# A graph layer's edge loop in which TensorE signals its results by a drain instead of by an increment at the product

## The reference

```
h = relu(layernorm(x))                                  # 12500 nodes x 128
rbf  = cut(d) * sin(k*pi*d/6) / (k*pi*d/6),  k = 1..8   # 200000 edges
w    = silu(silu(rbf @ fc_w1) @ fc_w2) @ fc_w3          # 4 x 32 weights for each edge
gs, gv = lin1(h)[src]                                   # gather: a row of 128 for each edge
msg  = [w00*gs*sh0, w11*(gv.sh1)/sqrt(3), w01*gs*sh1, w10*gv*sh0]    # 256 columns
agg  = segment_sum(msg, dst) / count                    # dst is sorted
out  = x + sc(h) + tanh(agg_s @ alpha_w) * lin2(agg)
```

## Time and profile before

| | |
|---|---|
| median of 3 timed runs | 2211.73 us (2203.23 to 2214.47) |
| profiled execution, first to last instruction | 2483.8 us |
| PE busy / weight loads busy | 1811.4 us (73%) / 1174.2 us (47%) |
| DVE busy | 1783.0 us (72%) |
| ACT busy | 1199.1 us (48%) |
| POOL busy | 1578.4 us (64%) |
| mean granted TensorE clock | 0.826 of 2.4 GHz |

### The profile page before, as it was taken

One profiled execution on the slowest core, in us unless ns is written; L12 is line 12 of the kernel. 1 busy time (PEld: TensorE's weight loads), 2 busy tenths in 40 slices (PEclk: granted clock), 3 DMA queues, 4 the chain that ended last, 5 costly groups with the idle time before them and its releaser, 6 DMA issues. The chain is left out here.

```text
span 2483.8 us, 34021 instructions
## 1 busy us (share of the span) xinstructions
PE 1811.4 (73%) x7969; PEld 1174.2 (47%) x7969; DVE 1783.0 (72%) x4669; ACT 1199.1 (48%) x3310; POOL 1578.4 (64%) x1624
## 2 busy tenths in 40 slices
PE   6577777787777777767677767667787776877777
PEld 6344444454444444444444434444554444544544
DVE  8577767767776777767676667767677776777777
ACT  6354545455454555444444344445444444445443
POOL 7566666666666666666666666666666666666563
PEclk9588878878888887788787878888888888888889
DMA  7322222222222222222122222222222222222222
GB/s 214 70 64 67 56 64 66 66 56 66 66 59 62 67 65 56 55 48 50 46 50 48 48 48 49 54 50 64 57 67 62 59 65 66 53 64 61 59 66 55
DMA packets 347699, 155.73 MB, mean 63 GB/s; under 512 B 237983, under 2 KB 322048, under 8 KB 347584
## 3 DMA queue, kind: packets, MB, share of 16 engines
q0 software_dynamic: 50016, 102.51, 15.7%
q1 hardware_dynamic: 296938, 51.75, 11.4%
q10 hardware_dynamic: 630, 0.29, 0.0%
HBM read 134.27 MB, written 20.15 MB: 62 GB/s over the span
## 5 line engine op out<-in xcount | busy, mean ns | idle before, releaser
L970 POOL DMA_INDIRECT lin_g<-lin_table,src_ix x1563 | 1530.0, 979 | 865.1 <-issue 441.5
L1157 ACT ACTIVATE lin_sh<-lin_g,harm 128x128 f32<-128x128 f32 x1563 | 483.8, 396 | 94.6 <-DMA lin_g<-lin_table,src_ix 87.6
L1040 PE MATMUL ps_sums<-near_sums,far_hot 128*128 128x257 f32 x520 | 208.0, 488 | 440.8 <-DVE agg L1474 206.0
L1030 PE MATMUL ps_near<-msg,onehot 128*64 128x257 f32 x3126 | 507.5, 471 | 1.2 <-DVE msg L1423 1.2
L1018 PE MATMUL ps_w<-w,h 128*128 128x256 f32 x1566 | 462.6, 440 | 28.2 <-ACT key_all L1167 18.5
L1018 PEld LDWEIGHTS ps_w<-w,h 128*128 128x128 f32 x1566 | 395.3, 272 | 135.4 <-issue 44.9
L999 PE MATMUL ps_h<-rbf,w 32*128 32x192 f32 x1044 | 277.0, 390 | 138.0 <-issue 67.1
L1415 DVE TENSOR_TENSOR msg<-lin_sh,key_all 128x576 f32<-128x576 f32 (+1 forms) x261 | 197.3, 756 | 249.9 <-ACT key_all L1167 209.5
L1167 ACT ACTIVATE key_all<-ps_w 128x768 f32<-128x768 f32 x261 | 213.5, 818 | 305.2 <-remote 188.6
L1030 PEld LDWEIGHTS ps_near<-msg,onehot 128*64 128x64 f32 x3126 | 241.3, 164 | 230.6 <-issue 175.7
L1383 DVE TENSOR_TENSOR lin_sh<-lin_g,ps_meta 128x576 f32<-128x576 f32 (+1 forms) x261 | 196.6, 753 | 212.2 <-DMA lin_g<-lin_table,src_ix 207.0
(11 more groups left out here) (175 smaller groups left out, 1655.2 us busy)
## 6 DMA issues: line engine op xcount, KB each, us to landing
lin_g<-lin_table,src_ix POOLq DMA_INDIRECT x1563
dist_in<-in_edge_weight SPq DMA_DIRECT2D x67, 96.0 KB
lin_table<-lin_out SPq DMA_DIRECT2D x24, 256.0 KB, 2.6
x_in<-in_x SPq DMA_DIRECT2D x24, 256.0 KB
skip_table<-x_in SPq DMA_DIRECT2D x24, 256.0 KB
xq<-in_x SPq DMA_DIRECT2D x23, 256.0 KB, 3.9
harm<-in_edge_attr SPq DMA_DIRECT2D x66, 48.0 KB
x_in<-skip_table SPq DMA_DIRECT2D x8, 256.0 KB
```

The costliest lines, as they stand in the source:

```text
L970: pool.indirect_dma_start(slot_tiles(s, u)[rows, t, :], None, lin_table, bass.IndirectOffsetOnAxis(ap=src_ix[rows, s.phase, u, col:col + 1 ...
L1030: mm = pe.matmul(ps_near[half * NEAR:(half + 1) * NEAR, 0:MSG + 1], onehot[:, u, t, :], msg[:, u % 2, t, :], start=(j == 0), stop=(j == PA ...
L1040: pe.matmul(ps_nodes(i), far_hot[:, u, :], near_sums[:, u % 2, :], start=True, stop=True).then_inc(sums_ready, 1)
L1157: last = act.activation(lin_sh0[:, u % 2, j, :], slot_tiles(s, u)[:, j, :], ACT.Copy, scale=harm[:, s.phase, u, harm_col(j):harm_col(j) + 1])
```

## The change

The five increments move from the last matmul of their part to a drain that follows it. Everything else stays: the products, their order, the waits, the semaphores and who waits for them. There are five drains for each group, 1305 in the edge loop. The order of the matmuls on TensorE, and of all instructions on the other engines, is the same as before.

```diff
@@ layer1
                             for part in range(2):
-                                mm = pe.matmul(ps_h1[:, part * SEG:(part + 1) * SEG], w1[rows, 2 * k + part, :], rbf[rows, :],
+                                pe.matmul(ps_h1[:, part * SEG:(part + 1) * SEG], w1[rows, 2 * k + part, :], rbf[rows, :],
                                                start=True, stop=True)
-                            mm.then_inc(h1_done, 1)
+                            pe.drain(fusable=False).then_inc(h1_done, 1)
@@ layer2
-                            pe.matmul(ps_h2[:, 0:UNIT], w2[:], h1[:, k % 2, :], start=True, stop=True).then_inc(h2_done, 1)
+                            pe.matmul(ps_h2[:, 0:UNIT], w2[:], h1[:, k % 2, :], start=True, stop=True)
+                            pe.drain(fusable=False).then_inc(h2_done, 1)
@@ layer3
                             for j in range(PAIRS):
-                                mm = pe.matmul(ps_w[:, 2 * j * P:(2 * j + 2) * P], cols[:, j, :], w3[:], start=True, stop=True)
-                            mm.then_inc(w_ready, 1)
+                                pe.matmul(ps_w[:, 2 * j * P:(2 * j + 2) * P], cols[:, j, :], w3[:], start=True, stop=True)
+                            pe.drain(fusable=False).then_inc(w_ready, 1)
@@ near_layer
-                                    mm = pe.matmul(ps_near[half * NEAR:(half + 1) * NEAR, 0:MSG + 1], onehot[:, u, t, :], msg[:, u % 2, t, :],
+                                    pe.matmul(ps_near[half * NEAR:(half + 1) * NEAR, 0:MSG + 1], onehot[:, u, t, :], msg[:, u % 2, t, :],
                                                    start=(j == 0), stop=(j == PAIRS - 1))
-                            mm.then_inc(near_ready, 1)
+                            pe.drain(fusable=False).then_inc(near_ready, 1)
@@ segment_sum
-                            pe.matmul(ps_nodes(i), far_hot[:, u, :], near_sums[:, u % 2, :], start=True, stop=True).then_inc(sums_ready, 1)
+                            pe.matmul(ps_nodes(i), far_hot[:, u, :], near_sums[:, u % 2, :], start=True, stop=True)
+                            pe.drain(fusable=False).then_inc(sums_ready, 1)
```

## The result

The changed kernel takes 2276.8 us (median of 4 runs, 2267.28 to 2281.96) against 2211.62 us of the kernel before (the median once a fourth run is counted): a ratio of 1.029, with a 95% interval of 1.026 to 1.0325, or 65 us more. The forecast was 2312 us, with 2120 to 2450 as its range.

The account below looks back on a forecast made before the run. POOL was taken to set the pace at full clock, PE at half clock. Uncovered half-clock drains (129 us) plus 10 us for late results, scaled by 0.89 and rounded down to 100, gave 2211.73 + 100 = 2312 us, range 2120 to 2450.

Parts of the forecast that it names:

- (a): PE's stream at full clock: drained parts no longer overlap, 5.40 us a group in place of 4.86, +0.54 us.
- (b): PE, ahead of layer3 and segment_sum: weight loads no longer run ahead of their products, +0.22 us a group.
- (c): PE, each drain: the drain itself and the sequencer's restart take 0.10 us, +0.5 us a group (0.2 to 1.5).
- 92 groups at half clock x 1.4 us: Edge loop: 92 of 261 groups run at half clock, where nothing covers the drains' 1.4 us each; 129 us.
- the loss sits at half clock: Edge loop: drains are hidden at full clock (4.9 to 6.1 us a group, under POOL's 7.5) and cost time at half clock.
- POOL as the cover: Edge loop at full clock: POOL's six gathers take 7.5 us a group and hide PE's longer group; cover 1.4 us.
- floor of 2051 us: POOL: 1563 gathers at 1.25 us make 1954 us, plus 68.1 us ahead of the first and 29.4 from the last's start.
- Rival 1: PE's signals arriving after their modelled end also slow timed runs, and drains end these late signals; 2130 us, chance 0.22.
- ACT's "remote" waits: Sign: ACT's idle waits ended by "remote" events, 342.1 and 188.6 us, should shrink if the signal comes from the sequencer.
- Rival 2: No change: PE runs nearly always at full clock and the 1.26 us hide behind POOL; 2205 to 2222 us, chance 0.11.
- Rival 3: Much slower: the drains' gaps cost PE its clock, half clock for 60% of the groups; 2555 us, chance 0.12.
- Rival 4: Drains' signals come as late as the increments did, with PE stopped meanwhile; timed runs as forecast, chance 0.55 shared with it.

Follow-up runs that it names:

- one_drain: Kernel before plus one silent drain an iteration, behind the last part of its fourth group, all increments left at the products; ratio 1.005 to the kernel before.
- layers_only: Kernel before with signalling drains behind layer1, layer2 and layer3 only; near_layer and segment_sum keep their increments at the products; ratio 1.033 to the kernel before.
- unpaced_before: Kernel before without POOL's waits for h2_done and sums_ready ahead of a group's third and fifth gather; 2181.5 us, ratio 0.986 to the kernel before.
- half_gather_before: Kernel before with all loop gathers but the first four groups' and the last fetching 64 of 128 rows; 2196.2 us, ratio 0.992 to the kernel before.
- layer2_twice: Kernel before with layer2's product issued twice into the same place, no drain; 2277.2 us, ratio 1.029 to the kernel before.

## Why the prediction was right, and where it was not

- **Direction and range: right.** Slower was given 0.66, and the time lies in the range, 35 us under the forecast.
- **(a) Parts end to end, +0.54 us: held.** In the changed kernel no product behind a drain starts less than 0.079 us after the modelled end of the one ahead.
- **(b) Weight loads in the open: held.** They start with their product. The first products of layer3 stretch its 1.46 us to 1.62 and those of segment_sum its 0.60 to 0.67: 0.23 us where 0.22 stood.
- **(c) 0.10 us for a drain and the restart: too small in two places.** The drain is 0.08 us. But ahead of segment_sum and of layer1 the gap is 0.22 us. There a second wait or register work stands in PE's list; in one_drain the next part starts 0.07 to 0.16 us before the modelled end all the same, so the sequencer did this while earlier products ran. The sum is 1.46 us at full clock instead of 1.26.
- **92 groups at half clock x 1.4 us: right in kind, with a wrong count.** The 1.4 us held: the distances between the parts at half clock make 10.93 us where they made 9.46 (the 9.40 us of the earlier trace rows is the length of the window), +1.47. The number of groups came from a disturbed execution. Undisturbed, 2 x (1 - 0.858) x 2226.0 = 632 us pass at half clock before, 67 groups, and 2 x (1 - 0.909) x 2280.2 = 415 us after, 38 groups. 38 x 1.47 = 56 us is near the 65 measured, but that is in part luck: the same product gives 49 us for layers_only, which costs 72.
- **Why 1.46 us x 261 = 381 us in PE's stream are only 65 us at the end.** PE's idle time from 100 us of the span on is nearly the same in both (466 and 448 us), but its gaps of more than 2 us sum up to 347 us in one_drain and to 166 in the changed kernel, and the stretches at half clock fell from 99 to 72. The 217 us less at half clock are worth at most half of that, some 109 us, and PE's wait for DVE's sum is 173.6 us shorter. Both are estimates of what is given back; they leave some 100 us where the spans differ by 54, so the account isn't closed. That it is the spread of the idle time that holds the clock is argued, not shown.
- **That the loss sits at half clock: only in part.** Sorting DVE's waits at L1416 (one_drain) and L1417 (changed) of over 0.1 us by the mean clock of the 7 us before them, those under 0.75 sum up to 54 us in one_drain and 73 after, those between to 38 and 62, those above 0.97 to 2 and 17. So 15 of the 58 us more fall where the prediction had the drains hidden.
- **POOL as the cover: wrong engine.** This step failed, though the time came out in the range. With POOL's two waits gone and with shorter gathers the drains cost 1.030 and 1.034, where a cover by POOL would have made them dearer (1.05 or more was expected). The loss shows on DVE, busy for 78 to 80% of the span, and PE gives up 173.6 us of its own wait for DVE. That these two are the cover is argued from the waits. The fastest kernel here still stands 130 us above the floor of 2051 us.
- **Rival 1 (faster) rested on the late signals, and these were no part of the kernel.** My reason for giving it little weight, that the profiled execution was 272 us longer than the median, was the right sign. None of the kernels run later shows a "remote" wait, three of them without any drain (unpaced_before, half_gather_before, layer2_twice). So that ACT's "remote" waits are gone in the changed kernel tells nothing of the drain, as I had thought it would.
- **Rival 2** fell with the result. **Rival 3** (the clock collapses) had the sign wrong: each kernel with more drains than one_drain has a higher clock. **Rival 4** fell: ACT's copy starts 0.06 us after the near products, with no late signal.
- **A slip in the range.** Its upper end is given as +215 us (92 x 2.4), which makes 221. Nothing hangs on it.

The Trainium skill (TensorE: Matmul & The Clock Gate, "What happens when you issue a matmul") made (a) about 0.85 us, an estimate. By the starts and modelled ends of this case's trace the overlap lost is 0.54 us, and the trace decides.

## What to carry to other kernels

A drain on TensorE costs little by itself, 0.08 us, but it takes away three kinds of cover: the overlap of parts, weight loads ahead of their products, and the sequencer's own work; together 0.3 us for each here. Leave the increment on the product. Dense work is no better than gaps here: one more product of layer2 a group cost as much as five drains. What a longer stream costs is read on the engine that waits for its result, here VectorE's two waits, and before a wait with an unknown releaser is made the reason for a change, look whether the profiled span fits the timed runs.

## What was not expected of the hardware

- A silent drain behind a product that signals (2299.5 us) is dearer than a drain that signals (2276.8 us). In its trace layer1 to layer2 are 1.014 us apart against 0.987: the drain ends 0.047 us after the product's modelled end where the increment hangs on the product, and 0.020 us after it where the drain itself signals. Why is open.
- The granted clock tended to rise with the number of stops: 0.858 (one_drain), 0.873 (one drain a group), 0.878 (two), 0.892 (three), 0.909 and 0.901 (five that signal, five silent), 0.918 (ten), though PE's products were the same. It isn't the stops alone: unpaced_before, with no drain, had 0.868, and layer2_twice, without stops but with more products, 0.897.
- In one profiled execution of the kernel before, more than half of TensorE's semaphore updates in the edge loop came over 0.3 us after the modelled end, many of them 1 to 6 us, with later products running meanwhile; in the first stage none did. Some 210 of the 1305 updates of the five parts are missing from its record as well. No other profiled execution here shows it, and what caused it stays open.
- Gathers that come as early as they can were better than paced ones: without POOL's two pacing waits the kernel before takes 2181.5 us, 1.4% less. It beats both kernels of this case.
